# Expert layers with the first weights as the stationary operand, and a mixer with two more TensorE passes a tile

## The chip, the cores and the metric

One core of a Trainium2 chip runs the whole program in one launch. The metric is the device time of a launch in microseconds (us). The kernel before took 2359.63 us in the median of three runs (2358.5 to 2360.95).

## The reference

A decoder of two layers works on 128 sequences of 64 tokens with 128 features, that is 8192 tokens, or 64 tiles of 128 tokens. Everything is float32. Layer 0 is causal self attention, cross attention and a mixture of eight experts of which each token takes two; layer 1 is a recurrent memory, a small mixer over the context and a mixture of eight experts of which each token takes one. Each part is added to its input and normalised. What the change touches is the two expert parts:

```python
# layer 0: top 2 of 8, F = 256 (two halves, W1 and W2), no biases
hidden = silu(x @ W1[e].T) * (x @ W2[e].T)          # 128 -> 256
y      = sum over the two experts of gate * (hidden @ W3[e].T)
# layer 1: top 1 of 8, DFF = 512
h1 = maximum(x @ W1[e] + b1[e], 0.0)                 # 128 -> 512
y  = gate * (h1 @ W2[e] + b2[e])                     # 512 -> 128
# layer 1's mixer, per sequence, on xm (tokens) and ctx (context):
h = ctx @ xm.T ; g = gelu(h) ; out = g.T @ ctx
```

## The kernel before, in words

The stages run one after another: self attention, cross attention (with the routing of layer 0's experts), layer 0's experts, the memory's products, its recurrence, memory and mixer (with the routing of layer 1's experts), layer 1's experts. Every stage is a pipeline written out by hand. Each engine runs its own program, `step(i)` is one tile's turn on it, and inside a step the engine works on tiles of different age (`t = i + 3`, `t = i + 2`, and so on). An engine executes its program strictly in order. Semaphores, which count finished tiles, tie the engines together: `pe.wait_ge(h_ready, t.count())` waits until the counter has reached tile t. Most buffers have two slots, so a writer also waits for the reader of two tiles before.

`run_experts` (line 976) is called once for each layer. The tokens were scattered into `tokens_by_expert`, so that each tile of 128 rows belongs to one expert: 144 tiles in layer 0 and 80 in layer 1. `experts_from` (line 983) loads the expert number of each tile into registers of the engine that asks, once every eight tiles. For a tile, in this order:

- TensorE transposes the 128 token rows (line 1109), and ScalarE copies the result from PSUM to `xt` (line 1144).
- TensorE multiplies with `xt` as the stationary side and 512 columns of first weights streaming past it (line 1115), so tokens come out on the partitions. In float32 each `matmul` is two passes in the profile.
- Layer 0: ScalarE applies Silu to one half (line 1150), VectorE multiplies by the other (line 1218) into `h`. Layer 1: VectorE adds the bias `b_up`, which stands on all 128 partitions as 8 x 512 numbers (line 1220).
- TensorE transposes `h` in two blocks (layer 0) or four (layer 1), line 1123; ScalarE copies them to `ht`, with Relu in layer 1 (line 1156).
- TensorE multiplies by the second weights, two or four times 128 columns (line 1131), and VectorE copies the result out, with the second bias in layer 1 (lines 1229, 1231). SyncE stores four tiles at a time.

In the second half of the tiles VectorE also does `combine` (line 1165) for tokens of the first half, in parts: parts 0 to 3 need the gathered expert outputs, part 4 gives the variance. GpSimd (line 1067) issues a root (line 1076) and then the next gathers, which are indirect transfers (line 1089).

`memory_and_mixer` (line 1708) has 64 tiles. TensorE's step has the order: logits (line 1843), output product (1849), `h` (1855), memory (1863), mix (1870), read (1877), two transposes (1887, 1888) and the transpose for the gate (1894). ScalarE's copy `yt` (line 1948) is what the logits of the same step's end wait for. In its tile 4, SyncE asks for layer 1's weights (lines 1759 to 1763); the first bias is sent to all 128 partitions, 2 MB in SBUF. Half way and at the end VectorE runs `route`, for which TensorE counts tokens into the PSUM bank `counts` (`count_tokens`, line 866).

Of the kernel before, what the change touches and what calls it, by code (L numbers as in the profile page):

```python
# [15 lines left out]
P = 128  # L16
# [777 lines left out]
class Experts:  # L794


    def __init__(self, nc, ctx, stage, a, top2, scattered, gathered):
# [12 lines left out]
        self.b_up = None if top2 else part(up + down, up, H_UP)  # L810
# [165 lines left out]
def run_experts(nc, f, k, xs, ys, x_out):  # L976
# [6 lines left out]
    def experts_from(engine):  # L983

        held = []

        def look(i):
            first, count = (0, 2) if i.c == -2 else (i.n, 8 if i.static and i.c + 10 > kind.ALL else 10)
            if i.c == -2 or i.c >= 0 and i.c % 8 == 0:
# [3 lines left out]
            at = i.c % 8 if i.c >= 0 else i.c  # L993
            return (held[at] if i.c >= 0 else None), (held[at + 2] if at + 2 < len(held) and i.c >= -2 else None)
        return look

    with ExitStack() as ctx:  # L997
# [6 lines left out]
        h = sb("h", [P, 2, HID])  # L1004
        ht = sb("ht", [P, 2, FC, P])
# [8 lines left out]
        xt_ps, up_ps, ht_ps, y_ps = ([ps(f"{n}{i}", [P, 512]) for i in range(2)] for n in ("xt", "up", "ht", "y"))  # L1014
# [4 lines left out]
        x_turned, x_copied, up_ready, silu_ready, h_ready, h_turned, h_copied, down_ready, y_copied = (  # L1019
            sem(n) for n in ("x_turned", "x_copied", "up_ready", "silu_ready", "h_ready", "h_turned", "h_copied", "down_ready", "y_copied"))  # L1020
# [76 lines left out]
        def _(pe):  # L1097
            look = experts_from(mybir.EngineType.PE)

            def step(i):  # L1100
                e_now, e_ahead = look(i)
# [9 lines left out]
                if t.exists():  # L1111
                    pe.wait_ge(x_copied, t.count())
                    if t.after(2):
                        pe.wait_ge(h_ready, t.count(less=2))
                    nc.tensor.matmul(up_ps[t.slot(2)][:, :], xt[:, t.slot(2), :], w_up[:, bass.ds(e_ahead, 1), :], start=True, stop=True)\  # L1115
                        .then_inc(up_ready, 1)
                t = i + 1
                if t.exists():
                    pe.wait_ge(h_ready, t.count())
                    if t.after(2):  # L1120
                        pe.wait_ge(h_copied, t.count(less=2))
# [3 lines left out]
                t = i  # L1125
                if t.exists():
                    pe.wait_ge(h_copied, t.count())
                    if t.after(2):
                        pe.wait_ge(y_copied, t.count(less=2))
                    for c in range(FC):  # L1130
                        mm = nc.tensor.matmul(y_ps[t.slot(2)][:, 0:D], ht[:, t.slot(2), c, :], w_down[:, bass.ds(e_now, 1), c, :],  # L1131
# [5 lines left out]
        def _(act):  # L1137
            def step(i):
                t = i + 3
# [6 lines left out]
                if t.exists() and top2:  # L1146
                    act.wait_ge(up_ready, t.count())
                    if t.after(2):
                        act.wait_ge(h_ready, t.count(less=2))
                    act.activation(act1[:, t.slot(2), :], up_ps[t.slot(2)][:, 0:HID], ACT.Silu).then_inc(silu_ready, 1)  # L1150
                t = i + 1
                if t.exists():
                    act.wait_ge(h_turned, t.count())
                    if t.after(2):
                        act.wait_ge(down_ready, t.count(less=2))
                    act.activation(ht[:, t.slot(2), :, :].rearrange("p c n -> p (c n)"), ht_ps[t.slot(2)][:, 0:HID],  # L1156
                                   ACT.Copy if top2 else ACT.Relu).then_inc(h_copied, 1)
# [3 lines left out]
        def _(dve):  # L1161
            look = experts_from(mybir.EngineType.DVE)
# [46 lines left out]
            def step(i):  # L1209
                e_now, e_ahead = (None, None) if top2 else look(i)  # L1210
                t = i + 2
                if t.exists():
                    s2 = t.slot(2)
                    dve.wait_ge(silu_ready if top2 else up_ready, t.count())
                    if t.after(2):
                        dve.wait_ge(h_turned, t.count(less=2))
                    if top2:
                        dve.tensor_tensor(h[:, s2, :], up_ps[s2][:, HID:2 * HID], act1[:, s2, :], ALU.mult).then_inc(h_ready, 1)  # L1218
                    else:
                        dve.tensor_tensor(h[:, s2, :], up_ps[s2][:, :], b_up[:, bass.ds(e_ahead, 1), :].rearrange("p a n -> p (a n)"), ALU.add)\  # L1220
                            .then_inc(h_ready, 1)
# [486 lines left out]
def memory_and_mixer(nc, stage, k, x_in, ctx_in, k_all, v_all, qt_all, eta_col, w_out_t, coef, offset, f, xs):  # L1708
# [4 lines left out]
    with ExitStack() as ctx:  # L1713
# [21 lines left out]
        yt = sb("yt", [P, 2, P])  # L1735
        m_ps, read_ps, out_ps, turn_ps, h_ps, mix_ps = (ps(n, [P, 512]) for n in ("m", "read", "out", "turn", "h", "mix"))
# [6 lines left out]
            [sem(f"{n}{j}") for j in range(2)] for n in ("summed", "stats_ready", "mean_ready", "var_ready", "rstd_ready", "normed"))  # L1743
        passed_dve, passed_pe, passed_pool = sem("passed_dve"), sem("passed_pe"), sem("passed_pool")
# [340 lines left out]
```

## Time and profile before

| | us |
|---|---|
| median of the runs | 2359.63 |
| the profiled execution's own time | 2369.03 |
| its span | 2367.3 |
| TensorE matmul busy (PE) | 1436.2 |
| TensorE weight load busy (PEld) | 1058.1 |
| VectorE busy (DVE) | 1457.6 |
| ScalarE busy (ACT) | 979.6 |
| GpSimd busy (POOL) | 1064.8 |

The profile is one execution. Times of its rows are microseconds from the start of the span, unless marked ns. PE and PEld are TensorE's matmuls and its loads of the stationary side, which overlap; the ends of matmuls are modelled, so starts are the better marks. PEclk is the granted TensorE clock as a share of 2.4 GHz: 1.00 or 0.50. In brackets stands the idle time of an engine before a row and what ended it. Layer 0's experts take the time from 785 to 1290 us (the last tile leaves TensorE at about 1178), the mixer from 1804 to 2046, layer 1's experts from 2048 to the end (last tile at about 2300).

### The profile page before, as it was taken

What the parts mean: (1) busy time and instruction counts of PE and PEld (TensorE: products, weight loads), DVE (VectorE), ACT (ScalarE), POOL (GpSimd) and SP (SyncE); (2) the same over time, 40 slices, a digit from 0 to 9 for tenths busy, and PEclk for the clock granted to TensorE, in tenths of its full rate; (3) what the DMA queues carried; (4) which work ended last, traced back from release to release, by engine and by line L of the source; (5) the groups of instructions that cost most, each with busy time, mean ns of one, the idle gap of its engine ahead of it and who ended that gap; (6) DMA issues with size and microseconds to landing.
All of it is one profiled execution on the core that took longest, in us unless ns stands there. A gap on an engine that the chain in (4) does not pass through costs nothing. (4 is left out here: it accounts for less than half of the span.)

```text
span 2367.3 us, 59279 instructions
## 1 busy us (share of the span) xinstructions
PE 1436.2 (61%) x17468; PEld 1058.1 (45%) x17500; DVE 1457.6 (62%) x5174; ACT 979.6 (41%) x2927; POOL 1064.8 (45%) x1607
## 2 busy tenths in 40 slices
PE   6999937998775329977701998000003767469870
PEld 4777725777564116644400775000002656257650
DVE  5999945888775203345543665699996586424555
ACT  4777725777463115533300554232234455123220
POOL 3666633555587650044373443233333347620236
PEclk9999977999897559989955999555555797679985
DMA  1222223111121112233321211200002312111222
GB/s 45 74 72 72 72 56 90 50 50 48 48 69 53 54 56 71 75 82 86 83 65 52 62 56 60 103 1 0 1 1 79 121 58 81 59 53 56 69 78 69
DMA packets 219329, 143.84 MB, mean 61 GB/s; under 512 B 22316, under 2 KB 207158, under 8 KB 218550
## 3 DMA queue, kind: packets, MB, share of 16 engines
q1 hardware_dynamic: 206902, 117.02, 17.0%
q0 software_dynamic: 12288, 25.19, 3.6%
q8 instruction: 59, 0.97, 0.2%
q14 instruction: 80, 0.66, 0.1%
HBM read 78.01 MB, written 55.67 MB: 56 GB/s over the span
## 5 line engine op out<-in xcount | busy, mean ns | idle before, releaser
L1089 POOL DMA_INDIRECT ffn_run_yg<-expert_outputs,ffn_source x192 | 184.4, 961 | 291.2 <-DMA expert_outputs<-ffn_run_y 226.1
L1115 PE MATMUL ffn_run_up_ps<-ffn_weights,ffn_run_xt 128*128 x448 | 255.2, 654 | 87.7 <-issue 51.2
L884 POOL DMA_INDIRECT tokens_by_expert<-ffn_x_all,ffn_dest x192 | 192.2, 1001 | 73.4 <-issue 47.0
L1832 PE MATMUL mixer_m_ps<-mixer_mine,mem_state_coef 128*64 128x64 f32 x4 | 0.5, 334 | 334.6 <-DVE mixer_off_in L1958 334.6
L1131 PE MATMUL ffn_run_y_ps<-ffn_weights,ffn_run_ht 128*128 x1216 | 184.1, 287 | 24.1 <-issue 18.4
L1131 PEld LDWEIGHTS ffn_run_y_ps<-ffn_weights,ffn_run_ht 128*128 128x128 f32 x1216 | 163.2, 202 | 27.9 <-issue 27.9
L1218 DVE TENSOR_TENSOR ffn_run_h<-ffn_run_up_ps,ffn_run_act 128x256 f32<-128x256 f32 x144 | 61.1, 424 | 169.8 <-ACT ffn_run_act L1150 140.1
L1156 ACT ACTIVATE ffn_run_ht<-ffn_run_ht_ps 128x256 f32<-128x256 f32 (+1 forms) x224 | 102.4, 457 | 143.4 <-PE ffn_run_ht_ps L1123 107.2
L1123 PEld LDWEIGHTS ffn_run_ht_ps<-k_ident,ffn_run_h 128*128 128x128 f32 x608 | 83.5, 149 | 167.6 <-issue 98.2
L1559 POOL TENSOR_TENSOR mem_state_coef<-recur_r2c,recur_half 128x1 f32<-128x1 f32 x64 | 68.4, 1069 | 185.9 <-DVE recur_r2c L1701 158.1
L1832 PEld LDWEIGHTS mixer_m_ps<-mixer_mine,mem_state_coef 128*64 128x64 f32 x4 | 0.3, 206 | 334.7 <-DVE mixer_ones L1956 334.7
L1144 ACT COPY ffn_run_xt<-ffn_run_xt_ps 128x128 f32<-128x128 f32 x224 | 59.5, 266 | 212.2 <-PE ffn_run_xt_ps L1109 87.4
L1123 PE MATMUL ffn_run_ht_ps<-k_ident,ffn_run_h 128*128 128x128 f32 x608 | 110.9, 288 | 30.3 <-DVE ffn_run_h L1220 15.3
L429 POOL TENSOR_TENSOR self_k_ex<-self_kt,k_head_mask 128x256 f32<-128x256 f32 x128 | 75.8, 613 | 116.3 <-ACT self_kt L646 116.3
L429 POOL TENSOR_TENSOR cross_k_ex<-cross_kt,k_head_mask 128x256 f32<-128x256 f32 x128 | 75.7, 611 | 97.4 <-ACT cross_kt L646 96.7
L1115 PEld LDWEIGHTS ffn_run_up_ps<-ffn_weights,ffn_run_xt 128*128 128x128 f32 x448 | 73.4, 206 | 97.3 <-issue 97.1
L1576 ACT ACTIVATE recur_var_new<-recur_h,recur_var,mem_state_coef 128x1 f32<-128x1 f32 x64 | 24.7, 387 | 213.7 <-DVE recur_h L1642 213.7
L1811 POOL TENSOR_TENSOR mixer_rstd<-mixer_ve,k_half 128x1 f32<-128x1 f32 x128 | 69.0, 552 | 95.0 <-DVE mixer_ve L1984 95.0
L1076 POOL TENSOR_TENSOR ffn_run_rstd<-ffn_run_ve,k_half 128x4 f32<-128x4 f32 x32 | 33.3, 1041 | 163.7 <-DVE ffn_run_ve L1197 163.3
L1150 ACT ACTIVATE ffn_run_act<-ffn_run_up_ps 128x256 f32<-128x256 f32 x144 | 55.3, 384 | 110.3 <-PE ffn_run_up_ps L1115 90.1
L1229 DVE COPY ffn_run_y<-ffn_run_y_ps 128x128 f32<-128x128 f32 x144 | 40.7, 283 | 86.9 <-remote 73.2
L1109 PE MATMUL ffn_run_xt_ps<-k_ident,ffn_run_x 128*128 128x128 f32 x224 | 65.8, 294 | 44.5 <-DMA ffn_run_x<-tokens_by_expert 34.0
(361 smaller groups left out, 4969.7 us busy)
## 6 DMA issues: line engine op xcount, KB each, us to landing
ffn_run_x<-tokens_by_expert SPq DMA_DIRECT2D x56, 256.0 KB
expert_outputs<-ffn_run_y SPq DMA_DIRECT2D x56, 256.0 KB, 2.4
tokens_by_expert<-fill_zeros SPq DMA_DIRECT2D x144, 64.0 KB, 1.6
memory_rows<-products_row SPq DMA_DIRECT2D x16, 390.0 KB, 4.2
ffn_weights<-memory_rows SPq DMA_DIRECT2D x4, 1560.0 KB, 9.9
self_x<-in_x SPq DMA_DIRECT2D x64, 64.0 KB, 1.8
self_xr<-in_x SPq DMA_DIRECT2D x64, 64.0 KB, 1.9
x<-self_y SPq DMA_DIRECT2D x64, 64.0 KB, 1.5
```

The source lines that it names most:

```text
L429: pool.tensor_tensor(k_ex[:, t.slot(2), b, :, :], kt[:, t.slot(2), b * S:(b + 1) * S].unsqueeze(1).to_broadcast([P, 4, S]), k["head_mask4" ...
L884: pool.indirect_dma_start(xs[t // HALF], bass.IndirectOffsetOnAxis(ap=self.dest[:, r, t:t + 1], axis=0), self.x_all[:, t, :], None)\
L1089: pool.indirect_dma_start(yg[:, g % 4, n, m, :], None, rows, bass.IndirectOffsetOnAxis(ap=f.source[:, m, 4 * g + n:4 * g + n + 1], axis=0))\
L1109: nc.tensor.transpose(xt_ps[t.slot(2)][:, 0:P], x[:, slot, t.c % 4, :], k["ident"][:, :]).then_inc(x_turned, 1)
L1115: nc.tensor.matmul(up_ps[t.slot(2)][:, :], xt[:, t.slot(2), :], w_up[:, bass.ds(e_ahead, 1), :], start=True, stop=True)\
L1123: tr = nc.tensor.transpose(ht_ps[t.slot(2)][:, c * P:(c + 1) * P], h[:, t.slot(2), c * P:(c + 1) * P], k["ident"][:, :])
L1131: mm = nc.tensor.matmul(y_ps[t.slot(2)][:, 0:D], ht[:, t.slot(2), c, :], w_down[:, bass.ds(e_now, 1), c, :], start=(c == 0), stop=(c == FC ...
L1144: act.copy(xt[:, t.slot(2), :], xt_ps[t.slot(2)][:, 0:P]).then_inc(x_copied, 1)
L1156: act.activation(ht[:, t.slot(2), :, :].rearrange("p c n -> p (c n)"), ht_ps[t.slot(2)][:, 0:HID], ACT.Copy if top2 else ACT.Relu).then_in ...
L1218: dve.tensor_tensor(h[:, s2, :], up_ps[s2][:, HID:2 * HID], act1[:, s2, :], ALU.mult).then_inc(h_ready, 1)
L1559: pool.tensor_tensor(coef[:, t:t + 1], v["r2c"], v["half"], ALU.pow).then_inc(root_ready, 1)
L1811: pool.tensor_tensor(rstd[n][:, s2, :], ve[n][:, s2, :], k["half"][:, 0:1], ALU.pow).then_inc(rstd_ready[n], 1)
```

## The change

1. In both expert parts the first product has its sides swapped: the expert's 512 weight columns are taken in four blocks of 128 as the stationary side, and `xt` streams past each. Hidden features come out on the partitions, in the order that the second product needs, so the transposes of `h` and the copies to `ht` are gone.
2. The stationary side is read from a new buffer `w_now` of two slots, which ScalarE fills from `w_up` with a copy of 128 x 512 numbers for each tile. For this ScalarE reads the expert numbers too. The copy for tile i + 3 stands in its step behind the Silu or Relu of tile i + 2.
3. Layer 1: VectorE adds the bias into `sums`, ScalarE applies Relu from `sums` into `h`. `h` has four slots in both layers.
4. The first bias is loaded as 32 rows of 128, transposed once by TensorE at the end of the mixer and kept as 32 columns.
5. In the mixer TensorE makes two more passes in each step (`spin`), of 512 bf16 columns into `counts`, which nobody reads. Half way TensorE waits until VectorE has read the counts.

The diff, cut to its core:

```diff
@@ run_experts: experts_from(engine, ahead), look(i) gives the register of tile i + ahead; TensorE 0, ScalarE 3, VectorE 2
+        sums = None if top2 else sb("sums", [P, 2, HID])
+        w_now = sb("w_now", [P, 2, H_UP])
+        h = sb("h", [P, 4, FC, P])
@@ tensor, step
                 t = i + 2
                 if t.exists():
                     pe.wait_ge(x_copied, t.count())
-                    if t.after(2):
-                        pe.wait_ge(h_ready, t.count(less=2))
-                    nc.tensor.matmul(up_ps[t.slot(2)][:, :], xt[:, t.slot(2), :], w_up[:, bass.ds(e_ahead, 1), :], start=True, stop=True)\
-                        .then_inc(up_ready, 1)
-                t = i + 1
...
-                    for c in range(FC):
-                        tr = nc.tensor.transpose(ht_ps[t.slot(2)][:, c * P:(c + 1) * P], h[:, t.slot(2), c * P:(c + 1) * P], k["ident"][:, :])
-                    tr.then_inc(h_turned, 1)
+                    pe.wait_ge(w_taken, t.count())
+                    if t.after(2):
+                        pe.wait_ge(h_ready if top2 else biased, t.count(less=2))
+                    for c in range(4):
+                        mm = nc.tensor.matmul(up_ps[t.slot(2)][:, c * P:(c + 1) * P], w_now[:, t.slot(2), c * P:(c + 1) * P], xt[:, t.slot(2), :],
+                                              start=True, stop=True)
+                    mm.then_inc(up_ready, 1)
@@ scalar, step, behind the copy of xt for i + 3
                 t = i + 2
+                if t.exists():
+                    if top2:
+                        act.wait_ge(up_ready, t.count())
...
+                        act.activation(act1[:, t.slot(2), :], up_ps[t.slot(2)][:, 0:HID], ACT.Silu).then_inc(silu_ready, 1)
+                    else:
+                        act.wait_ge(biased, t.count())
...
+                        act.activation(h[:, t.slot(4), :, :].rearrange("p c n -> p (c n)"), sums[:, t.slot(2), :], ACT.Relu).then_inc(h_ready, 1)
+                t = i + 3
+                if t.exists():
+                    act.copy(w_now[:, t.slot(2), :], w_up[:, bass.ds(e_ahead, 1), :].rearrange("p a n -> p (a n)")).then_inc(w_taken, 1)
@@ vector, step, layer 1
+                        dve.tensor_tensor(sums[:, s2, :].rearrange("p (c n) -> p c n", n=P), up_ps[s2][:, :].rearrange("p (c n) -> p c n", n=P),
+                                          b_up[:, bass.ds(e_ahead, 1), :].rearrange("p a c -> p (a c)").unsqueeze(2).to_broadcast([P, 4, P]), ALU.add)\
+                            .then_inc(biased, 1)
@@ memory_and_mixer, sync
-                    sp.dma_start(f.b_up[:, :, :].rearrange("p e h -> p (e h)"),
-                                 f.a["b1"].rearrange("(a e) h -> a (e h)", a=1).to_broadcast([P, E_N * H_UP])).then_inc(f.weights_in, 16)
+                    sp.dma_start(raw_b[:, :], f.a["b1"].rearrange("e (c f) -> (e c) f", f=P)).then_inc(f.weights_in, 16)
@@ memory_and_mixer, tensor
+            def spin():
+                nc.tensor.matmul(counts[:, :], k["ident_bf"][:, :], k["causal"][:, :, :], start=True, stop=True)
+
             def step(i):
+                spin()
...
+                spin()                      # between the read product and the two transposes
...
+            def between():
+                f.count_tokens(pe, counts, 0)
+                pe.wait_ge(f.counts_read, 1)
+            half_way(pe, step, 6, 3, Eights, middle, between)
+            pe.wait_ge(f.weights_in, 64)
+            pe.wait_ge(summed[0], NT)
+            nc.tensor.transpose(out_ps[:, 0:4 * E_N], raw_b[:, :], k["ident"][0:4 * E_N, 0:4 * E_N]).then_inc(bias_turned, 1)
             f.count_tokens(pe, counts, 1)
```

## Rows read from the trace of the kernel before

**Rows 1.** Windows of engines: stretch, length, busy us of each (instructions), PEclk, DMA, GB/s.
```profile
880.00:1000.00 120.00, 114.15 (x601) 75.57 (x602) 41.68 (x134) 61.66 (x201) 0.00 (x0) 0.99 0.27 74
...
2095.00:2185.00 90.00, 90.00 (x571) 68.43 (x571) 37.35 (x78) 32.72 (x77) 0.00 (x0) 0.98 0.20 57
...
1957.00:1977.00 20.00, 17.56 (x74) 15.56 (x75) 11.16 (x53) 8.81 (x34) 12.69 (x20) 0.50 0.30 92
```

**Rows 2.** Timeline, layer 0's experts: start, duration, engine, line, operation, [idle before].
```profile
931.59 1.02 PE L1115 MATMUL ffn_run_up_ps<-ffn_weights,ffn_run_xt 128*128 x2
...
932.45 0.38 PE L1123 MATMUL ffn_run_ht_ps<-k_ident,ffn_run_h 128*128 128x128 f32 x2
...
932.65 0.38 ACT L1150 ACTIVATE ffn_run_act<-ffn_run_up_ps 128x256 f32<-128x256 f32 x1 [0.59 <-PE ffn_run_up_ps L1115]
...
932.93 0.38 ACT L1156 ACTIVATE ffn_run_ht<-ffn_run_ht_ps 128x256 f32<-128x256 f32 x1
...
933.22 1.02 PE L1115 MATMUL ffn_run_up_ps<-ffn_weights,ffn_run_xt 128*128 x2
```

**Rows 3.** Timeline, the same stage, a first product that had to wait, and its Silu.
```profile
940.83 1.12 PE L1115 MATMUL ffn_run_up_ps<-ffn_weights,ffn_run_xt 128*128 x2
...
942.06 0.38 ACT L1150 ACTIVATE ffn_run_act<-ffn_run_up_ps 128x256 f32<-128x256 f32 x1 [0.84 <-PE ffn_run_up_ps L1115]
```

**Rows 4.** Timeline, layer 1's experts, one tile on TensorE and VectorE.
```profile
2119.41 1.02 PE L1115 MATMUL ffn_run_up_ps<-ffn_weights,ffn_run_xt 128*128 x2
2120.28 0.60 PE L1123 MATMUL ffn_run_ht_ps<-k_ident,ffn_run_h 128*128 128x128 f32 x4
2120.60 0.69 DVE L1220 TENSOR_TENSOR ffn_run_h<-ffn_run_up_ps,ffn_weights 128x512 f32<-128x512 f32 x1 [0.68 <-PE ffn_run_up_ps L1115]
2120.71 1.06 PE L1131 MATMUL ffn_run_y_ps<-ffn_weights,ffn_run_ht 128*128 x8
...
2121.61 0.27 PE L1109 MATMUL ffn_run_xt_ps<-k_ident,ffn_run_x 128*128 128x128 f32 x1
```

**Rows 5.** Groups by shape, ScalarE: count | busy us, mean ns | idle before.
```profile
L664 ACT ACTIVATE cross_prob<-cross_prob 128x1024 f32<-128x1024 f32 x64 | 67.8, 1059 | 6.4 <-DVE cross_prob L719 6.1
...
L1156 ACT ACTIVATE ffn_run_ht<-ffn_run_ht_ps 128x512 f32<-128x512 f32 x80 | 47.8, 597 | 117.0 <-PE ffn_run_ht_ps L1123 96.2 <-remote 14.4 <-PE ffn_run_y_ps L1131 5.4
```

**Rows 6.** Timeline, layer 1's experts, ScalarE with a 512 wide operation and the next.
```profile
2094.30 0.60 ACT L1156 ACTIVATE ffn_run_ht<-ffn_run_ht_ps 128x512 f32<-128x512 f32 x1
...
2094.79 0.27 ACT L1144 COPY ffn_run_xt<-ffn_run_xt_ps 128x128 f32<-128x128 f32 x1
```

**Rows 7.** Timeline, mixer at full clock: ScalarE's copy, and the logits of two steps.
```profile
1893.50 0.27 ACT L1948 COPY mixer_yt<-mixer_gate_ps 128x128 f32<-128x128 f32 x1
...
1893.82 0.39 PE L1843 MATMUL mixer_gate_ps<-ffn_w_gate,mixer_yt 128*128 128x8 f32 x2 [0.52 <-ACT mixer_yt L1948]
...
1896.47 0.39 PE L1843 MATMUL mixer_gate_ps<-ffn_w_gate,mixer_yt 128*128 128x8 f32 x2 [0.52 <-ACT mixer_yt L1948]
```

**Rows 8.** Timeline, mixer at half clock, the logits of two steps.
```profile
1962.67 0.60 PE L1843 MATMUL mixer_gate_ps<-ffn_w_gate,mixer_yt 128*128 128x8 f32 x2 [0.42 <-ACT mixer_yt L1948]
...
1966.65 0.60 PE L1843 MATMUL mixer_gate_ps<-ffn_w_gate,mixer_yt 128*128 128x8 f32 x2 [0.42 <-ACT mixer_yt L1948]
```

**Rows 9.** Timeline, GpSimd's roots in the second halves of both expert stages.
```profile
1057.25 1.05 POOL L1076 TENSOR_TENSOR ffn_run_rstd<-ffn_run_ve,k_half 128x4 f32<-128x4 f32 x1 [9.23 <-DVE ffn_run_ve L1197]
...
1077.65 1.04 POOL L1076 TENSOR_TENSOR ffn_run_rstd<-ffn_run_ve,k_half 128x4 f32<-128x4 f32 x1 [9.41 <-DVE ffn_run_ve L1197]
...
2246.08 1.04 POOL L1076 TENSOR_TENSOR ffn_run_rstd<-ffn_run_ve,k_half 128x4 f32<-128x4 f32 x1 [13.40 <-DVE ffn_run_ve L1197]
...
2270.66 1.03 POOL L1076 TENSOR_TENSOR ffn_run_rstd<-ffn_run_ve,k_half 128x4 f32<-128x4 f32 x1 [12.47 <-DVE ffn_run_ve L1197]
```

**Rows 10.** Timeline, mixer: SyncE's request for the first bias, TensorE's wait behind it.
```profile
1823.14 12.84 SPq L1761 DMA_DIRECT2D ffn_weights<-in_L_ffn_b  x1
...
1849.30 0.48 PE L1887 MATMUL mixer_turn_ps<-k_ident,mixer_c 128*128 128x128 f32 x1 [8.35 <-DMA mixer_c<-in_ctx]
```

More of the change, by code:

```diff
@@ L809, in __init__ @@
         self.w_down = self.weights[:, up:up + down].rearrange("p (e c m) -> p e c m", c=self.FC, m=P)
-        self.b_up = None if top2 else part(up + down, up, H_UP)
+        self.b_up = None if top2 else part(up + down, E_N * 4, 4)
         self.b_down = None if top2 else part(2 * up + down, E_N * D, D)
@@ L981, in run_experts, with experts_from @@
     w_up, w_down, b_up, b_down, expert_of, x_all, gate = f.w_up, f.w_down, f.b_up, f.b_down, f.expert_of, f.x_all, f.gate
-    def experts_from(engine):
+    def experts_from(engine, ahead):
         held = []
         def look(i):
-            first, count = (0, 2) if i.c == -2 else (i.n, 8 if i.static and i.c + 10 > kind.ALL else 10)
-            if i.c == -2 or i.c >= 0 and i.c % 8 == 0:
+            if i.c < -ahead:
+                return None, None
+            early = i.c < 0
+            if early and i.c == -ahead or not early and i.c % 8 == 0:
+                first = 0 if early else i.n
+                count = ahead if early else min(8 + ahead, kind.ALL - i.c) if i.static else 8 + ahead
                 held[:] = nc.values_load_multi_w_load_instructions(
@@ L992, in look @@
                     skip_runtime_bounds_check_because="route() counts at most seven")[1]
-            at = i.c % 8 if i.c >= 0 else i.c
-            return (held[at] if i.c >= 0 else None), (held[at + 2] if at + 2 < len(held) and i.c >= -2 else None)
+            if early:
+                return None, held[i.c + ahead]
+            at = i.c % 8
+            return held[at], (held[at + ahead] if at + ahead < len(held) else None)
         return look
@@ L1013, in run_experts @@
         out = sb("out", [P, 2, 4, D])
-        xt_ps, up_ps, ht_ps, y_ps = ([ps(f"{n}{i}", [P, 512]) for i in range(2)] for n in ("xt", "up", "ht", "y"))
+        xt_ps, up_ps, y_ps = ([ps(f"{n}{i}", [P, 512]) for i in range(2)] for n in ("xt", "up", "y"))
         loaded = [sem(f"x_loaded{i}") for i in range(2)]
@@ L1120, in step @@
                     if t.after(2):
[L1121 to L1128 removed]
                         pe.wait_ge(y_copied, t.count(less=2))
                     for c in range(FC):
[L1131 removed]
+                        mm = nc.tensor.matmul(y_ps[t.slot(2)][:, 0:D], h[:, t.slot(4), c, :], w_down[:, bass.ds(e_now, 1), c, :],
                                               start=(c == 0), stop=(c == FC - 1))
@@ L1137, in _ @@
         def _(act):
+            look = experts_from(mybir.EngineType.Activation, 3)
             def step(i):
+                e_ahead = look(i)[1]
                 t = i + 3
@@ L1145, in step @@
                 t = i + 2
[L1146 to L1151, printed above, removed]
-                if t.exists():
[L1153 to L1157, printed above, removed]
+                if t.exists():
+                    if top2:
+                        act.wait_ge(up_ready, t.count())
+                        if t.after(2):
+                            act.wait_ge(h_ready, t.count(less=2))
+                        act.activation(act1[:, t.slot(2), :], up_ps[t.slot(2)][:, 0:HID], ACT.Silu).then_inc(silu_ready, 1)
+                    else:
+                        act.wait_ge(biased, t.count())
+                        if t.after(4):
+                            act.wait_ge(down_ready, t.count(less=4))
+                        act.activation(h[:, t.slot(4), :, :].rearrange("p c n -> p (c n)"), sums[:, t.slot(2), :], ACT.Relu).then_inc(h_ready, 1)
+                t = i + 3
+                if t.exists():
+                    act.copy(w_now[:, t.slot(2), :], w_up[:, bass.ds(e_ahead, 1), :].rearrange("p a n -> p (a n)")).then_inc(w_taken, 1)
             skewed(act, step, 3, 0, kind)
@@ L1950, in _ @@
             f.exponentials(act, 1)
+            act.wait_ge(bias_turned, 1)
+            act.copy(f.b_up.rearrange("p e c -> p (e c)"), out_ps[:, 0:4 * E_N]).then_inc(bias_copied, 1)
+            act.wait_ge(bias_copied, 1)
         @block.vector
```

30 lines of the change are left out of this document (16 added, 14 removed).

## The prediction

> **What bounds the kernel now.** I read the profile stage by stage, since the stages run one after another: first the windows of the engines for stretches of even work, then the timeline of one tile in each, then the groups by shape for the price of operations that would be new. In both expert stages the first half of the tiles is bound by TensorE itself: it is busy 114.15 of 120 us in layer 0 and 90.00 of 90 us in layer 1, at a granted clock of 0.99 and 0.98, while VectorE and ScalarE have about half their time free [rows 1]. A tile of layer 0 is 9 TensorE instructions, so the 601 in the window are 66.8 tiles, 1.80 us each; the pure rhythm is 933.22 - 931.59 = 1.63 us [rows 2], and what comes on top is a gap once in eight tiles, where the loop turns and the expert numbers are loaded. In layer 1 it is 15 instructions a tile, 571 / 15 = 38.1 tiles, 2.36 us each. In the second halves eight tiles take longer, 1077.65 - 1057.25 = 20.4 us in layer 0 and 2270.66 - 2246.08 = 24.6 us in layer 1 [rows 9], because the gathers hold engines up. In the mixer a tile takes 1896.47 - 1893.82 = 2.65 us at full clock [rows 7] and 1966.65 - 1962.67 = 3.98 us at half clock [rows 8].
>
> **The change part by part: what TensorE saves.** Four transposes of `h` in layer 1 last from 2120.28 to the start of the next group at 2120.71, 0.43 us or 0.107 each [rows 4]. So TensorE loses 0.21 us a tile in layer 0 and 0.43 in layer 1. The first product streams as many columns as before: two passes of 512 last 0.87 us (2119.41 to 2120.28), and eight passes of 128 with a load each, which the second product of layer 1 already is, last 2121.61 - 2120.71 = 0.90 us [rows 4]. I add 0.03 us. If TensorE stayed the bound, layer 0's tile would take about 1.45 us and layer 1's 1.9.
>
> On this product a rule of the Trainium skill can be weighed ("TensorE: Matmul & The Clock Gate", section "Back-to-back issue gap"): in a stream of load and matmul pairs the spacing is set by both, and it gives about 81 ns for 128 columns and 131 ns for 512. By the ratio of these figures four blocks would cost 2.5 times one wide pass, an estimate of 0.87 x 2.5 = 2.2 us for the product in place of 0.90. The trace has the same pattern of 128 column passes at 0.11 us a pass and doesn't bear that out for float32; the row decides.
>
> **What takes TensorE's place.** Follow ScalarE's program. It does Silu (or Relu) of tile i + 2, and only then copies the weights for tile i + 3. TensorE's first product of tile i + 3 waits for that copy. But Silu of i + 2 waits for the first product of i + 2. So first product, Silu, copy, next first product form one ring, and a second slot of `w_now` doesn't open it, because the order in ScalarE's queue closes it. Its length in layer 0: from the start of a first product that had to wait to its Silu 942.06 - 940.83 = 1.23 us [rows 3]; from Silu's start to the start of the next operation on ScalarE 932.93 - 932.65 = 0.28 [rows 2]; the copy, of which the trace has no example (512 wide, SBUF to SBUF). Bounds: a 512 wide operation from PSUM takes 0.597 us, one of 1024 from SBUF takes 1.059 [rows 5], so it lies above half of that, 0.53, and hardly above 0.65. I take 0.61, by the row nearest in shape. From the end of a ScalarE copy to TensorE's start 1893.82 - 1893.77 = 0.05 [rows 7], and 0.03 for the passes. Sum 2.20 us against 1.63. In layer 1 VectorE's add and the Relu stand in the ring: 1.19 us to the add (2120.60 - 2119.41) [rows 4], with 0.1 more for a product that had to wait (1.12 against 1.02 busy) [rows 3], 0.69 for the add, 0.05 to ScalarE, 0.49 from a 512 wide operation to the next (2094.79 - 2094.30) [rows 6], 0.61 for the copy, 0.05: 3.18 us against 2.30. The second product and the transpose of the tokens (0.56 us in layer 0, 1.0 in layer 1) lie beside the ring, in the time in which TensorE waits; so does the loading of expert numbers on TensorE, and mostly ScalarE's new one, which falls beside a running product. I leave 0.05 us a tile for it. The copies to `ht` (0.38 and 0.60) go, and nothing gains by that: they were not in a ring.
>
> Layer 0, first half: 67 tiles x (2.25 - 1.80) = +30 us. The tiles before it crawl while GpSimd scatters, at the pace of something other than these engines' work; I cost them at nothing. Second half, 72 tiles: in seven periods of eight tiles a gather of 10 us falls in. Now the tiles take 8 x 1.63 = 13 of the 20.4 us and the rest is the hold. With the slower ring they take 8 x 2.25 = 18 and part of the hold is hidden: if all but what it takes now at the least is hidden, the period stays about 20.4, if none is, it is 25. I take 22.4, +2 us seven times, +14. The other 16 tiles cost 0.45 to 0.6 each, +8. Layer 0: +52 us, between +35 and +70.
>
> Layer 1, first half: 36 tiles at full pace x (3.23 - 2.36) = +31. Second half: three periods in which VectorE waits for gathers that are issued after its own part 4. From a root to the landing of two groups of gathers is some 15 us, and the next four tiles to the next part 4 now take the rest of 24.6; in the new rhythm four tiles take 12.9, so 28 in all, +3 each or +9. Some 13 other tiles at 0.87 give +11. Layer 1: +51 us, between +40 and +70.
>
> **The mixer.** The first bias no longer goes to 128 partitions: SyncE's request for it held its queue for 12.84 us, and TensorE waited 8.35 us for context that was asked for behind it [rows 10]. Gone is most of that wait; late next are the two other weight transfers of 2 MB each, so I take -7, between -8.35 and 0. The first `spin` falls before the logits, where TensorE waits 0.52 us for ScalarE anyway [rows 7]: nothing, at either clock nearly. The second stands between the read product and the transposes, and ScalarE's copies and so the next logits hang on these: 512 columns in one pass, as half of the first product's 0.87 us is an upper bound at full clock (float32), and 0.2 us the value that I take since 128 columns of one pass take 0.107 and bf16 has not more passes than float32; bounds 0.1 and 0.44. Some 45 tiles at full clock: +10. Against it stands the clock: the tiles at half clock lose 3.98 - 2.65 = 1.33 us each, five of them between 1957 and 1977 although TensorE is busy 17.56 of 20 us there [rows 1, 8], and I expect as many again around the weight transfer. Passes without gaps may bring the full clock earlier; bounds 0 and -13, I take -7. Transposing the bias at the end and the wait half way cost TensorE nothing that VectorE's routing chain doesn't cover. Mixer: -4 us, between -20 and +20.
>
> **Sum.** 52 + 51 - 4 = +99 us on the profiled execution's own 2369.0 (span 2367.3), 2468. The runs lie 9.4 us below the profiled one, so 2459; I say 2460.
>
> **The rivals.** (a) The clock falls in the expert stages. TensorE would stream 1.4 of 2.2 us in layer 0 and 1.85 of 3.2 in layer 1. For it: the mixer ran at half clock at 88% busy for 20 us [rows 1]. Against it: the mixer's tile at full clock also streams little over half of its 2.65 us and stays there. At half clock the ring grows by the product's 0.87 us: for some 110 tiles +95, so 2555. The Trainium skill says in the same page, Part 1, that the throttled clock is the default and activity releases it; rows here show both outcomes. (b) The hold by gathers hides nearly all of the slower ring, and ScalarE's copy is at its lower bound (0.53): layer 0 +35, layer 1 +35, mixer -15, so 2415. (c) The other side: TensorE stays the bound, because the ring is shorter than its own work. Then it saves 0.21 x 144 + 0.43 x 80 less 0.03 x 224 = 58 us and the mixer 4, so 2298. It would need a copy that costs nothing: layer 0's ring without it is 1.59 us, hardly below the 1.63 of today, and it decides from there. Only if ScalarE's part overlaps in a way that its program order forbids does this happen. (d) The gains and losses of the mixer are all that is seen since ring and gap cancel: 2355 to 2365, no change.
>
> **How the numbers follow.** Forecast (clock stays, ring sets the pace) 0.70, with its own range 2425 to 2500; (a) 0.13; (b) 0.10; (c) 0.05; (d) 0.02. A change of 0.2% is about what can be told from none here. Range 2410 to 2515: it takes in (b), the forecast with the bounds of the copy and the second halves, and a clock that falls in part. Slower 0.93, same 0.02, faster 0.05.
>
> **What would show it.** Right: on TensorE a wait before nearly every first product, ended by ScalarE's copy; rhythm 2.2 us and 3.2 us a tile in the first halves, TensorE busy well below its 114 of 120 us; copies of about 0.61 us; the second halves slower by less; the mixer without the 8.35 us wait. Wrong: first products that start right behind the transpose of the tokens; a copy below 0.3 us; PEclk at 0.5 in the expert stages (then a); or a stage outside these three that moves.

## The result, and the profile after

The changed kernel takes 2469.49 us in the median of four runs (2466.65 to 2472.75); the kernel before, run beside it, 2360.29. The ratio is 1.0466, with a 95% interval from 1.0447 to 1.0485: 4.7% slower. Forecast were 2460 us and +99 us on the profiled execution; the spans differ by 2464.9 - 2367.3 = 97.6 us. The medians differ by 109.2 us: the profiled execution of the kernel before lies 9.4 us above its median, the changed kernel's 2.8 below. The table and all stages below compare single executions.

The stages are marked off by TensorE's first token transpose of each expert part and its first product of the mixer. Differences to before:

| stage | before, us | after, us | measured | forecast |
|---|---|---|---|---|
| up to layer 0's experts | 791.96 | 788.63 | -3.3 | 0 |
| layer 0's experts, products, recurrence | 1013.55 | 1073.98 | +60.4 | +52 |
| mixer | 245.98 | 232.18 | -13.8 | -4 |
| layer 1's experts | 315.81 | 370.11 | +54.3 | +51 |

First the windows of the first halves, which answer to [rows 1]: TensorE (first number) was busy 114.15 of 120 and 90.00 of 90 us, and now has 25.5 and 31.6 us free, at the same granted clock.

```profile
880.00:1000.00 120.00, 94.50 (x709) 81.97 (x709) 34.24 (x110) 58.46 (x164) 0.00 (x0) 0.99 0.20 57
2160.00:2250.00 90.00, 58.41 (x466) 52.66 (x465) 26.54 (x54) 35.41 (x81) 0.00 (x0) 1.00 0.14 39
```

A tile is now 13 instructions in layer 0 and 17 in layer 1, so these are 54.5 tiles of 2.20 us and 27.4 of 3.28 us. The timeline of one round of the ring in layer 0 answers to [rows 2, 3]: copy, first product, Silu, next copy.

```profile
935.36 0.61 ACT L1164 COPY ffn_run_w_now<-ffn_weights 128x512 f32 x1
...
936.07 1.13 PE L1124 MATMUL ffn_run_up_ps<-ffn_run_xt,ffn_run_w_now 128*128 128x128 f32 x8 [0.47 <-issue]
...
937.24 0.38 ACT L1156 ACTIVATE ffn_run_act<-ffn_run_up_ps 128x256 f32<-128x256 f32 x1 [1.10 <-PE ffn_run_up_ps L1124]
937.52 0.61 ACT L1164 COPY ffn_run_w_now<-ffn_weights 128x512 f32 x1
```

From copy to copy it is 937.52 - 935.36 = 2.16 us. And in layer 1, which answers to [rows 4, 6], where VectorE's add stands in it too:

```profile
2168.60 0.60 ACT L1164 COPY ffn_run_w_now<-ffn_weights 128x512 f32 x1
...
2169.30 1.13 PE L1124 MATMUL ffn_run_up_ps<-ffn_run_xt,ffn_run_w_now 128*128 128x128 f32 x8 [1.19 <-issue]
...
2170.59 0.69 DVE L1231 TENSOR_TENSOR ffn_run_sums<-ffn_run_up_ps,ffn_weights 128x512 f32<-128x512 f32 x1 [2.14 <-PE ffn_run_up_ps L1124]
...
2171.31 0.63 ACT L1161 ACTIVATE ffn_run_h<-ffn_run_sums 128x512 f32<-128x512 f32 x1 [1.95 <-DVE ffn_run_sums L1231]
...
2171.85 0.60 ACT L1164 COPY ffn_run_w_now<-ffn_weights 128x512 f32 x1
```

2171.85 - 2168.60 = 3.25 us. The groups of the page give the price that the trace of before did not have, the copy's 607 ns. The list of TensorE's waits from 900 to 1000 (us in total, times, longest) shows 46 waits before first products, about one a tile, and names "issue" for 40 of them. The name is misleading: in the round above the product starts 0.10 us after the copy's end (936.07 against 935.36 + 0.61), and e1, e2 and e4 below show that the copy is what it waits for.

```profile
L1124 PE MATMUL ffn_run_up_ps<-ffn_run_xt,ffn_run_w_now 128*128 128x128 f32 x1792 | 276.5, 301 | 294.2 <-issue 278.7
L1164 ACT COPY ffn_run_w_now<-ffn_weights 128x512 f32 x224 | 136.1, 607 | 0.0
```
```profile
PE ffn_run_up_ps L1124 <- issue: 19.3, 40, 0.6
PE ffn_run_up_ps L1124 <- ACT ffn_run_w_now L1164: 2.0, 6, 0.4
```

GpSimd's roots in layer 0's second half answer to [rows 9], and the rows of one eight-tile period, in order of time, show the hold:

```profile
1118.21 1.04 POOL L1083 TENSOR_TENSOR ffn_run_rstd<-ffn_run_ve,k_half 128x4 f32<-128x4 f32 x1 [13.27 <-DVE ffn_run_ve L1204]
...
1142.31 1.04 POOL L1083 TENSOR_TENSOR ffn_run_rstd<-ffn_run_ve,k_half 128x4 f32<-128x4 f32 x1 [13.04 <-DVE ffn_run_ve L1204]
```
```profile
1106.74 0.38 ACT L1156 ACTIVATE ffn_run_act<-ffn_run_up_ps 128x256 f32<-128x256 f32 x1 [5.92 <-remote]
1107.02 0.61 ACT L1164 COPY ffn_run_w_now<-ffn_weights 128x512 f32 x1
...
1107.73 2.04 PE L1124 MATMUL ffn_run_up_ps<-ffn_run_xt,ffn_run_w_now 128*128 128x128 f32 x8 [6.14 <-issue]
...
1110.80 1.45 PE L1124 MATMUL ffn_run_up_ps<-ffn_run_xt,ffn_run_w_now 128*128 128x128 f32 x8
...
1113.27 1.13 PE L1124 MATMUL ffn_run_up_ps<-ffn_run_xt,ffn_run_w_now 128*128 128x128 f32 x8 [0.47 <-issue]
```
```profile
1107.70:1110.70 3.00, 2.97 (x13) 2.74 (x13) 1.44 (x6) 0.98 (x3) 0.00 (x0) 0.50 0.00 0
```

ScalarE stands first, for 5.92 us before a Silu whose product was done, and "remote" names no cause; TensorE's product starts 0.10 us after ScalarE's next copy, so TensorE's 6.14 us are the ring again. From the first product before the stop, at 1099.88, to the next are 7.85 us, 5.7 more than a round of 2.16. Behind it PEclk is 0.50 for 3 us and the next two tiles take 3.07 and 2.47 us, 0.9 and 0.3 more. Together these are 6.9 us, the whole hold.

In the mixer SyncE is still held for 12.16 us at the request for the bias, though only 32 rows are asked for, and TensorE's longest wait for context is 5.6 us where it was 8.35 [rows 10]:

```profile
1881.10 12.16 SPq L1775 DMA_DIRECT2D mixer_raw_b<-in_L_ffn_b  x1
```
```profile
PE mixer_turn_ps L1905 <- DMA mixer_c<-in_ctx: 6.3, 3, 5.6
```

### The profile page after: what moved, and what is told of

It reads as the page before. It is cut to its first block and busy times, and to the rows that moved or that the text cites. A ratio compares the mean times of both kernels' runs of the same rounds, so it can differ in the third digit from the quotient of the medians.

```text
span 2464.9 us, 60850 instructions
## 1 busy us (share of the span) xinstructions
PE 1407.7 (57%) x18328; PEld 1121.7 (46%) x18383; DVE 1455.5 (59%) x5174; ACT 1038.6 (42%) x3009; POOL 1066.2 (43%) x1607
## 5 line engine op out<-in xcount | busy, mean ns | idle before, releaser
L1124 PE MATMUL ffn_run_up_ps<-ffn_run_xt,ffn_run_w_now 128*128 128x128 f32 x1792 | 276.5, 301 | 294.2 <-issue 278.7
L1124 PEld LDWEIGHTS ffn_run_up_ps<-ffn_run_xt,ffn_run_w_now 128*128 128x128 f32 x1792 | 237.5, 206 | 343.5 <-issue 332.7
L1133 PE MATMUL ffn_run_y_ps<-ffn_weights,ffn_run_h 128*128 x1216 | 182.4, 286 | 0.4 <-DVE ffn_run_y L1241 0.4
L1133 PEld LDWEIGHTS ffn_run_y_ps<-ffn_weights,ffn_run_h 128*128 128x128 f32 x1216 | 163.8, 203 | 0.7 <-issue 0.6
L1231 DVE TENSOR_TENSOR ffn_run_sums<-ffn_run_up_ps,ffn_weights 128x512 f32<-128x512 f32 x80 | 55.3, 691 | 160.4 <-PE ffn_run_up_ps L1124 136.9
L1164 ACT COPY ffn_run_w_now<-ffn_weights 128x512 f32 x224 | 136.1, 607 | 0.0
L1161 ACT ACTIVATE ffn_run_h<-ffn_run_sums 128x512 f32<-128x512 f32 x80 | 50.4, 629 | 173.7 <-DVE ffn_run_sums L1231 146.2
L1588 ACT ACTIVATE recur_var_new<-recur_h,recur_var,mem_state_coef 128x1 f32<-128x1 f32 x64 | 24.7, 387 | 213.7 <-DVE recur_h L1654 213.7
L1183 DVE SCALAR_TENSOR_TENSOR ffn_run_r<-ffn_run_yg,ffn_gate,ffn_x_all 128x128 f32<-128x128 f32 x128 | 43.6, 341 | 74.7 <-DMA ffn_run_yg<-expert_outputs,ffn_source 74.6
L706 DVE TENSOR_REDUCE cross_top<-cross_s_ps_ps 128x16 f32<-128x1024 f32 x64 | 77.7, 1214 | 17.0 <-PE cross_s_ps_ps L519 15.3
```

Source lines behind the costliest of these rows:

```text
L706: dve.tensor_reduce(top[:, t.slot(2), :].rearrange("p (q h) -> p q h", q=4), s_ps, AX, ALU.max).then_inc(top_ready, 1)
L1124: mm = nc.tensor.matmul(up_ps[t.slot(2)][:, c * P:(c + 1) * P], w_now[:, t.slot(2), c * P:(c + 1) * P], xt[:, t.slot(2), :], start=True, s ...
L1133: mm = nc.tensor.matmul(y_ps[t.slot(2)][:, 0:D], h[:, t.slot(4), c, :], w_down[:, bass.ds(e_now, 1), c, :], start=(c == 0), stop=(c == FC ...
L1164: act.copy(w_now[:, t.slot(2), :], w_up[:, bass.ds(e_ahead, 1), :].rearrange("p a n -> p (a n)")).then_inc(w_taken, 1)
L1231: dve.tensor_tensor(sums[:, s2, :].rearrange("p (c n) -> p c n", n=P), up_ps[s2][:, :].rearrange("p (c n) -> p c n", n=P), b_up[:, bass.ds ...
```

## The experiments

### The ring: opened, emptied, lengthened

**e1_copy_first** moves the copy within ScalarE's step:

```diff
                     act.copy(xt[:, t.slot(2), :], xt_ps[...]).then_inc(x_copied, 1)
+                    act.copy(w_now[:, t.slot(2), :], w_up[:, bass.ds(e_ahead, 1), :]...).then_inc(w_taken, 1)
                 t = i + 2
                 ... Silu, or Relu
-                t = i + 3
-                if t.exists():
-                    act.copy(w_now[...], ...).then_inc(w_taken, 1)
```

> The changed kernel with ScalarE's copy of the weights of tile i + 3 moved ahead of its Silu or Relu of tile i + 2. Theory (the order in ScalarE's program closes a ring of first product, Silu or add and Relu, copy, next first product): the ring opens, TensorE is the bound again at about 1.5 us a tile in layer 0 (2.15 now) and 1.95 in layer 1 (3.25 now). First halves 67 x 0.65 + 36 x 1.3 = 90 us, second halves some 60 more where the gathers don't hold: 2290 to 2340, below the kernel before. Rival (the four block product, its weight loads or the register loads on ScalarE set the rhythm, wherever the copy stands): within 10 us of the changed kernel's 2469.

Measured: 2312.49 us (2309.91 to 2313.2), ratio to before 0.9815 (0.9791 to 0.9839). One line moved takes 157 us off, and of the kernels that leave nothing out this is the fastest. Windows of its first halves (the end of the first one reaches into the first stop by gathers), then TensorE's timeline in layer 0:

```profile
880.00:1000.00 120.00, 110.36 (x943) 106.50 (x942) 44.67 (x143) 81.53 (x214) 9.45 (x10) 0.98 0.30 84
2080.00:2140.00 60.00, 58.12 (x514) 57.20 (x512) 29.31 (x61) 39.17 (x90) 0.00 (x0) 1.00 0.23 65
```
```profile
942.14 1.06 PE L1124 MATMUL ffn_run_up_ps<-ffn_run_xt,ffn_run_w_now 128*128 128x128 f32 x8
943.03 0.61 PE L1133 MATMUL ffn_run_y_ps<-ffn_weights,ffn_run_h 128*128 x4
943.48 0.27 PE L1116 MATMUL ffn_run_xt_ps<-k_ident,ffn_run_x 128*128 128x128 f32 x1
943.59 1.06 PE L1124 MATMUL ffn_run_up_ps<-ffn_run_xt,ffn_run_w_now 128*128 128x128 f32 x8
```

In these rows TensorE has no gap left. A tile of layer 0 takes 943.59 - 942.14 = 1.45 us, just what the prediction gave for a TensorE that stays the bound, and the product lasts 943.03 - 942.14 = 0.89 us, against 0.87 in two wide passes. The prediction weighed a rule of the Trainium skill here ("TensorE: Matmul & The Clock Gate", "Back-to-back issue gap"), by whose ratio it estimated 2.2 us for four blocks; this run measures 0.89, so that ratio doesn't hold for these float32 passes.

**e2_no_copy** takes copy, waits and expert numbers away:

```diff
-                    pe.wait_ge(w_taken, t.count())
-                        ... w_now[:, t.slot(2), c * P:(c + 1) * P], xt[...]
+                        ... w_up[:, 0, c * P:(c + 1) * P], xt[...]
```

> The changed kernel without ScalarE's copy and without its loads of expert numbers: the first product takes its four stationary blocks from expert 0's weights for every tile (it leaves out the choice of the expert in the first product). It measures the four block product alone. Theory: no ring, TensorE is the bound, 2280 to 2320, and the first product lasts 0.9 to 1.0 us from its start to the next group's. Rival (the block product itself is dear): a first product of over 1.5 us and 2400 or more.

Measured: 2294.27 us (2289.67 to 2295.74), ratio 0.9736. The block product costs no more than before, and a copy out of the ring costs at most 18 us more than none.

**e4_copy_twice** lengthens the ring:

```diff
+                    act.copy(w_spare[:, t.slot(2), :], w_up[:, bass.ds(e_ahead, 1), :]...)
                     act.copy(w_now[:, t.slot(2), :], w_up[:, bass.ds(e_ahead, 1), :]...).then_inc(w_taken, 1)
```

> The changed kernel with a second copy of the same size ahead of the one that counts, into a buffer that nobody reads. Theory (the copy stands whole in the ring): +0.6 us a tile in the first halves, 103 x 0.6 = +62, and as the hold by gathers was seen to hide nearly nothing of a longer ring, about as much per tile in the second halves, some 105 x 0.55 = +58: +120, 2590. Rival (the gathers hide a slower ring, as the prediction took by half): +90. Rival (no ring): +0 to +20.

Measured: 2558.78 us (2556.89 to 2563.13), +89 on the changed kernel. The forecast of +120 missed, and the first rival's +90 was met: the gathers hid a part. Where no gather runs, eight tiles grew from 17.2 to 21.4 us, 0.52 a tile, as the timeline of ScalarE has it: the second copy starts 0.51 us after the first.

```profile
937.03 0.61 ACT L1165 COPY ffn_run_w_spare<-ffn_weights 128x512 f32 x1
937.54 0.62 ACT L1166 COPY ffn_run_w_now<-ffn_weights 128x512 f32 x1
```

With gathers, a period grew only from 24.1 to 26.5 us, where eight tiles without them grew by 4.1: the hold shrank from 6.9 to 5.1 us, so part of this second lengthening was hidden.

### The second halves: what the hold hangs on

Eight tiles with a gather and eight without, from the roots of layer 0 in each trace: before 20.4 and 13.3, after 24.1 and 17.2, e1_copy_first 19.5 and 11.8. The hold is the difference: 7.1, 6.9 and 7.7 us. It varies by about 1 us from program to program: e3_no_spins and e9_mixer_no_spins below, with the same expert code as the changed kernel, have periods of 23.1 and 23.0 us on average, and 17.2 without a gather. **e8_quarter_gathers** makes the gathers small, **e11_plain_loads** makes them plain:

```diff
@@ e8_quarter_gathers
-   pool.indirect_dma_start(yg[:, ...], None, rows, ...(ap=f.source[:, ...]))
+   pool.indirect_dma_start(yg[0:(P if g < 4 else 32), ...], None, rows, ...(ap=f.source[0:(P if g < 4 else 32), ...]))
@@ e11_plain_loads, for g >= 4
+   pool.dma_start(yg[:, g % 4, n, m, :], rows[(4 * g + n) * P:(4 * g + n + 1) * P, :]).then_inc(gathered[g % 4], 16)
```

> The changed kernel with every gather after the first four groups of a layer fetching 32 rows in place of 128 (it leaves out three quarters of the rows); the number of gathers, their order and GpSimd's instructions stay. It tells what the hold of about 7 us in each eight tiles of layer 0's second half hangs on. Theory (on the rows that the gathers move): the periods fall from 24 us towards the 17.2 us of eight tiles without a gather, 2415 to 2435. Rival (on issuing the gathers, which GpSimd and the instruction fetch do whatever the size): periods stay at 23 to 24, within 10 us of 2469.

Measured: 2479.68 us (2478.4 to 2480.22), 10 more than the changed kernel. The periods stayed at 23.5 to 24.7 us and TensorE's stops were the same, 6.1 us in five of six periods and 4.7 in one (in the changed kernel likewise):

```profile
1156.85 2.05 PE L1124 MATMUL ffn_run_up_ps<-ffn_run_xt,ffn_run_w_now 128*128 128x128 f32 x8 [6.13 <-issue]
```

> The changed kernel with every gather after the first four groups of a layer replaced by a plain load of 128 consecutive rows of the same size, asked for by GpSimd at the same place (it leaves out the choice of the rows). With a quarter of the rows the hold of eight tiles had stayed at 7 us (e8_quarter_gathers: periods of 24.1 to 24.5), so it doesn't hang on the bytes. Theory (it hangs on the indirect form): periods of eight tiles fall to 17.2 to 19 us, and where GpSimd's 11.1 us a group set the pace behind the last tile, those shrink too: 2300 to 2400 in all. Rival (any transfer that GpSimd asks for in that loop brings the hold, or it comes from the code of the loop itself): periods stay at 23 us or more in the tiles.

Measured: 2381.49 us (2378.79 to 2384.39), 88 less than the changed kernel. Roots of GpSimd's timeline, where the plain loads have begun:

```profile
1120.37 1.04 POOL L1083 TENSOR_TENSOR ffn_run_rstd<-ffn_run_ve,k_half 128x4 f32<-128x4 f32 x1 [12.31 <-DVE ffn_run_ve L1207]
1121.38 4.41 POOL L1101 DMA_DIRECT2D ffn_run_yg<-expert_outputs  x8
1137.85 1.03 POOL L1083 TENSOR_TENSOR ffn_run_rstd<-ffn_run_ve,k_half 128x4 f32<-128x4 f32 x1 [12.06 <-DVE ffn_run_ve L1207]
```

1137.85 - 1120.37 = 17.5 us in place of 24: the stop is gone. Of the 88 us this is the smaller part: between the same roots of the last five periods layer 0 took 25.7 us less, and behind its last tile 40.9 less, where a group of gathers takes 11.1 us and one of plain loads some 6. So the hold belongs to the indirect form of a transfer as GpSimd issues it, not to its bytes. The plain form also keeps GpSimd for 4.4 us in place of some 10, and no run separates that time from the form. Why ScalarE stands still for 6 us, and TensorE behind it, stays open.

### The mixer: the bias and the spins

**e5_wide_bias** puts a broadcast of 1.8 MB back in front of the small load, on e1_copy_first.

```diff
+                    sp.dma_start(f.b_wide..., f.a["b1"][0:E_N - 1, :]....to_broadcast([P, (E_N - 1) * H_UP])).then_inc(f.weights_in, 16)
                     sp.dma_start(raw_b[:, :], ...)
```

> e1_copy_first with the broadcast of the first bias to all partitions loaded as well (seven of eight experts, 1.8 MB, into columns that nobody reads), ahead of the small load. It undoes the bias part of the change and leaves all else. Theory (the wide load takes queue and DMA time from the context that the mixer's TensorE waits for): the mixer stage grows from 235.7 us by 3 to 12 us and the kernel with it, 2315 to 2325. Rival (SyncE is held for 12 us by the two 2 MB weight loads whichever bias load stands behind them, and nothing is lost): within 3 us of e1_copy_first's 2312.

Measured: 2320.3 us (2317.38 to 2323.6), 8 more than e1_copy_first, though the ratios to before, 0.9847 (0.9823 to 0.9872) and 0.9815 (0.9791 to 0.9839), have intervals that just overlap; the mixer grew from 235.7 to 241.3 us. TensorE's waits for the context, e1_copy_first:

```profile
PE mixer_turn_ps L1903 <- DMA mixer_c<-in_ctx: 7.8, 2, 7.0
```

and with the wide bias:

```profile
PE mixer_turn_ps L1905 <- DMA mixer_c<-in_ctx: 13.4, 2, 12.9
```

12.9 - 7.0 = 5.9 us is about the mixer's growth of 5.6. SyncE is held in both, 13.7 us and 14.6 us, but the context behind it comes later when 1.8 MB more are ahead. The other traces agree: with the wide bias TensorE's longest wait for context is 8.35 (before), 12.9 (e5, e10) and 13.0 us (e7), with the small one it lies between 4.8 and 8.0 us in nine traces.

**e3_no_spins** (on the changed kernel) and **e6_first_no_spins** (on e1_copy_first) were to leave out the spins of the mixer. Their edit took more than their expectations say, namely the three spins a tile in the memory products as well, which the kernel before has too:

```diff
@@ memory_products, tensor, three places
-                spin()
@@ memory_and_mixer, tensor, two places
-                spin()
```

> The changed kernel with both spins of the mixer left out (the smaller bias load stays). Theory (spins cost next to nothing, since a loop over the other engines sets the 2.65 us, and they keep the clock up): the mixer loses what the clock gave, +3 to +10 us. Rival (each second spin costs 0.2 us on the path, the price of the prediction): -5 to -10 us.

> e1_copy_first without both spins of the mixer. Theory (a loop over the other engines sets the mixer's 2.65 us a tile, with or without spins): the mixer stage stays at 235 +- 4 us. The whole time then follows, 2312 +- 5, unless the clock of another stage falls differently, as in e3_no_spins, where the memory products ran all their 210 us at half clock with nothing changed in them; that would show as 30 to 40 us in that stage alone. Rival (spins keep the clock up in the mixer): the mixer stage grows by 5 to 20 us.

Measured: 2509.97 us (2498.39 to 2513.26), +40, and 2360.29 us (2352.96 to 2366.17), +48. Windows of the memory products, e1_copy_first and then e6_first_no_spins:

```profile
1300.00:1460.00 160.00, 148.80 (x1349) 104.66 (x1348) 101.54 (x491) 79.76 (x334) 61.20 (x165) 0.97 0.21 66
```
```profile
1300.00:1460.00 160.00, 160.00 (x1017) 126.53 (x1016) 92.94 (x438) 71.11 (x290) 53.92 (x146) 0.50 0.17 53
```

Without those spins TensorE is busy 160 of 160 us at a PEclk of 0.50, and from the last root of layer 0's tiles to the mixer it takes 38 us more (668.96 against 631.18; e3_no_spins 670.31, the changed kernel 631.56). e6's expectation put e3's half clock down to the stage itself; that was wrong, the spins in it were missing.

**e7_before_spins** put one spin a tile into the mixer of the kernel before, and the other by mistake into the memory products. **e10_before_spins** has both at the change's places, and **e9_mixer_no_spins** takes just these two from the changed kernel:

```diff
@@ e10_before_spins, memory_and_mixer, tensor (e9_mixer_no_spins takes the two calls away)
             def step(i):
+                spin()
...
+                spin()                      # between the read product and the two transposes
```

> The kernel before with the two spins a tile in the mixer and the wait half way, and nothing else of the change. Theory (spins take the place of idle time): within 4 us of before in the mixer's full clock stretches, 2.65 us a tile; where the clock had fallen (1957 to 1977) up to 7 us are won: -7 to +3. Rival (the second spin costs 0.2 us of the path a tile, as predicted): +3 to +9.

> The kernel before with both spins a tile in the mixer and the wait half way, at the places that the change gives them (e7_before_spins had the second one in the memory products, where it cost 5 us). Theory (spins take the place of idle time, and where the clock had fallen they bring it back): the mixer stage falls from 246.0 us to 236 to 242, as in e7_before_spins with 237.7, and the kernel by 4 to 10 us, 2347 to 2353. Rival (0.2 us a tile for the second spin): 2357 to 2366.

> The changed kernel without the two spins a tile of the mixer alone. The edits of e3_no_spins and e6_first_no_spins had also taken the three spins a tile of the memory products, which the kernel before has too, and those stages ran at half clock. Theory (a loop over the other engines sets the mixer's 2.65 us a tile): the memory products stay at full clock, the mixer stage at 232 to 242 us (232.2 with spins), the kernel at 2469 to 2479. Rival (the second spin costs 0.2 us a tile): 2460.

Measured: e7 2359.69 us (ratio to before 1.0011, 0.9993 to 1.0028), mixer 237.7; e10 2347.71 us (0.9984, 0.9972 to 0.9995), mixer 241.3; e9 2464.47 us, ratio 1.0468 (1.0450 to 1.0486) where the changed kernel had 1.0466, mixer 244.9. So taking the mixer's spins out changes nothing in the whole time that can be measured (e9's mixer is 12.7 us longer, but its stages from layer 0's experts to the mixer, with the same code, are 10.0 shorter), and putting them in gains 4 us; no run shows the +10 that was forecast. The mixers without any spin took 231.9 (e3), 242.3 (e6) and 244.9 us (e9), those with both spins and the small bias 232.2, 235.7, 232.9, 235.2, 232.8 and 233.5.

The traces show two effects of the spins. The clock comes back earlier. These windows of 12 us begin just behind the longest wait for context, first the kernel before and e10_before_spins, then e9_mixer_no_spins and the changed kernel:

```profile
1850.00:1862.00 12.00, 10.68 (x46) 9.51 (x45) 5.69 (x27) 5.59 (x21) 2.87 (x6) 0.50 0.21 66
1847.00:1859.00 12.00, 11.22 (x63) 8.52 (x62) 6.44 (x32) 6.16 (x25) 3.66 (x8) 0.80 0.22 68
```
```profile
1892.00:1904.00 12.00, 10.68 (x46) 9.48 (x47) 5.12 (x25) 5.33 (x20) 2.86 (x6) 0.50 0.22 66
1901.00:1913.00 12.00, 10.90 (x63) 8.75 (x63) 6.27 (x32) 6.12 (x25) 3.57 (x8) 0.76 0.21 66
```

Without spins the mixer has nine (before), seven (e9) and seven (e6) steps of about 4 us, with one or both of them at most one in each of nine traces. e3, without spins, has none either: there the wait is 4.8 us, the shortest, and its profiled execution is the fastest of five. And at full clock the second spin costs a little: from the 21st to the 44th tile both spins take 62.1 to 62.2 us in all eight traces that have them, none or only the first takes 60.2 to 60.4 in five, which is 0.08 us a tile.

## Why the prediction was right

**The ring.** Confirmed as a mechanism by e1, e2 and e4, and term by term: 1.17 us to Silu (forecast 1.23), 0.28 to the copy (0.28), 0.61 for the copy (0.61), 0.10 to the next product (0.05 + 0.03): 2.16 against 2.20. Layer 1: 1.29, 0.69 + 0.03, 0.54, 0.60, 0.10: 3.25 against 3.18. What was left for register loads, 0.05 a tile, is the rest up to 2.20 and 3.28 in the windows.

**First halves.** Forecast +30 and +31. To the first root layer 0 lost 35.6 us, of which one period with a gather, and layer 1 lost 47.3 up to the root that was at 2220.63, where the forecast had 31 and most of the 11 for single tiles.

**The gathers of layer 0: the term that was off.** I had taken a period from 20.4 to 22.4, half of the longer ring hidden in the hold. It went to 24.1, +3.7, where the tiles alone grew by 17.2 - 13.3 = 3.9: hidden was 0.2. From the first to the last root of the tiles that is +25.5 us, against 6 x 2 + 4 = 16 by the forecast's steps. The hold, 5.7 us of stop and 1.2 us of low clock behind it, comes on top of the tiles' time, and in e11 it goes with the indirect transfers. By its upper bound of 25 the prediction had this case in the range, not in the sum. In e4 part was hidden, so it isn't a law.

**Layer 1's three periods.** Before 25.5, 24.6 and 26.2, after 29.1, 27.5 and 26.3: +6.7, forecast +9 and 28 each.

**The mixer.** Forecast -4, measured -13.8. Its mis-sized terms are the spin and the clock. The second spin starts 0.21 us before the transpose, as priced, yet the rhythm here is 1925.43 - 1922.77 = 2.66 us against 2.65 [rows 7], and 0.08 a tile dearer by the traces above, some +4 us in place of +10. The wait of 0.52 us before the logits has shrunk to 0.31, so the spins mostly eat idle time:

```profile
1924.21 0.38 PE L1853 MATMUL mixer_counts_ps<-k_causal,k_ident_bf 128*128 128x512 bf16 x1
1924.42 0.27 PE L1905 MATMUL mixer_turn_ps<-k_ident,mixer_c 128*128 128x128 f32 x1
...
1925.43 0.39 PE L1860 MATMUL mixer_gate_ps<-ffn_w_gate,mixer_yt 128*128 128x8 f32 x2 [0.31 <-ACT mixer_yt L1973]
```

And SyncE's 12.84 us did not come from the bias: the request behind the two weight loads waits whatever it asks for. The -7 was near what e5 shows (-5.6), for another reason than the one given; between the two profiled executions the wait itself shrank by 2.7 us. The clock was to give -7: nine steps at half clock are gone, 9 x 1.33 = 12 us by an estimate from [rows 7, 8], near the bound of -13. With +4 and -2.7 that makes -11 of the -13.8; the rest is open. The wait half way cost nothing: the two longest steps there are 21.2 us before, 21.2 in e9 and 19.6 in the changed kernel.

**The sum.** That it came within 2 us of the spans' 97.6 is luck in part: layer 0 missed by +8.4, layer 1 by +3.3, the mixer by -9.8 and the stages ahead of layer 0's experts by -3.3, which cancel. The ring, which carries most of the loss, was not luck.

**The rivals.** (a) fell: PEclk stayed at 0.99 and 1.00 in the first halves; behind each stop of the second half it was low for some 3 us. (b), 2415, fell on the hold and on a copy of 0.607, not 0.53. (c), 2298, is what the kernel does as soon as the ring is open: e2_no_copy took 2294 and e1_copy_first 2312. Its mechanism, ScalarE's part overlapping, needed another program order, as said. (d) fell with the two stages of over 50 us each.

## What to carry to other kernels

A buffer with two slots doesn't decouple two engines if one engine's program puts the refill behind work that waits for the consumer: draw the ring through program order, and move the refill ahead of the instruction that waits. When a hold shares a stage with a longer loop, look at where it stops the engines before calling it cover; here the slower loop was added to it almost whole. Extra passes into idle time of TensorE cost little in the rhythm (0.08 us a tile in the mixer, where one lasts 0.21) and can bring the full clock back earlier; those in the memory products are what keeps that stage at full clock. Compare stages over several traces before pricing a few us: with the same code one stage differed by 10 us between two programs.

## What the hardware showed that was not expected

TensorE busy without a gap for 160 us stayed at PEclk 0.50 (e6_first_no_spins), and the mixer of the same kernel, busy 15.69 of 20 us, ran at 1.00:

```profile
1920.00:1940.00 20.00, 15.69 (x114) 12.96 (x113) 16.00 (x77) 12.82 (x54) 10.56 (x22) 1.00 0.25 79
```

The Trainium skill says in "TensorE: Matmul & The Clock Gate", Part 1, that activity releases the throttled clock. In this trace the stage's passes without a gap did not release it, and with three bf16 spins a tile between them they did, so a busy share of 100% in the profile is no proof of full clock. That the passes are float32 is not enough to explain it: layer 1's experts of the kernel before, float32 too and busy 90.00 of 90 us, ran at 0.98 [rows 1]. What in the memory products' passes differs was not tested.

In the changed kernel eight indirect transfers of GpSimd bring a stop of about 6 us on ScalarE, and on TensorE behind it, whether they fetch 128 or 32 rows each; in the kernel before the stops of TensorE were 3.3 to 4.1 us. Eight plain loads bring none, and take GpSimd 4.41 us in place of some 10.
